# Keys turned inside the recurrence, expert choice and indirect stores inside the mixing

## What is computed

```python
q, k, v = (short_conv(x @ W.T, w) for W, w in ...)      # four taps, then silu
beta = sigmoid(x @ Wb.T)
q, k = l2norm(q), l2norm(k); v = v * beta; kb = k * beta
A = tril(-(kb @ k.T), -1)                               # chunks of 32 in the reference
T = inverse of (I - A), row by row
u, w = T @ v, T @ kb
# recurrence: u_i = u - w @ S; o = q @ S + tril(q @ k.T) @ u_i; S = S + k.T @ u_i
paths = (short_fir(v), long_fir(v), delta, v)
hmid = gelu([x, mean and variance of each path and head] @ W1.T + b1)
probs = softmax(hmid @ W2.T ...), floored, normed
out = rmsnorm(sum of probs * paths) @ Wo.T
x = layernorm(x + out)
logits = x @ router_w + router_b                        # top 2 of 8, softmax over the two
x = layernorm(x + sum over the two of weight * expert(x))
```

## Time and profile before

| | us |
|---|---|
| median of 3 runs | 1947.79 (1944.25 to 1954.17) |
| profiled execution | 1950.38, span of its instructions 1948.6 |
| middle stage in it | about 240 to 1430 |
| one pair of its loop, 1054.6 to 1190.4 | 135.8 |
| busy in this pair | PE 114.1, DVE 111.9, ACT 73.9, POOL 20.7 |

### The profile page before, as it was taken

The page is one execution under the profiler, slowest core; times in us unless marked ns, Lnnn a source line. Parts: engine busy times, 40 slices in busy tenths (PEclk is TensorE's granted clock), DMA queues, the critical chain, the costliest instruction groups (busy, mean ns, idle before and its releaser), DMA issues. The chain is left out here.

```text
span 1948.6 us, 40303 instructions
## 1 busy us (share of the span) xinstructions
PE 1461.2 (75%) x12217; PEld 1100.7 (56%) x12218; DVE 1352.0 (69%) x3875; ACT 948.0 (49%) x1990; POOL 443.0 (23%) x473
## 2 busy tenths in 40 slices
PE   6776075877979789789789789687419999999800
PEld 3446044746738658567467467485307777777700
DVE  6995064778878887887878888875574444444488
ACT  5771160455545654655555465432344444444434
POOL 5784200000030040130210300302042333333300
PEclk9997585987987988889879879867659999999955
DMA  5548732033253233333333332431535533333295
GB/s 190 193 162 239 185 66 52 12 74 84 58 130 97 63 103 98 88 88 108 85 100 87 110 86 66 108 98 61 168 113 162 160 94 95 96 93 95 74 368 195
DMA packets 297373, 224.36 MB, mean 115 GB/s; under 512 B 173472, under 2 KB 265632, under 8 KB 296960
## 3 DMA queue, kind: packets, MB, share of 16 engines
q1 hardware_dynamic: 225600, 158.84, 28.7%
q0 software_dynamic: 15232, 43.53, 6.2%
q10 hardware_dynamic: 56384, 19.93, 4.4%
HBM read 130.42 MB, written 91.82 MB: 114 GB/s over the span
## 5 line engine op out<-in xcount | busy, mean ns | idle before, releaser
L2019 POOL DMA_INDIRECT y_d<-C_yb,C_dest x136 | 131.6, 968 | 260.1 <-ACT C_yb L2130 257.5
L1443 DVE SCALAR_TENSOR_TENSOR B_conv<-B_ps_x,B_cw,B_conv 128x511 f32<-128x511 f32 (+2 forms) x192 | 143.4, 747 | 39.6 <-ACT B_conv L1161 34.6
L688 POOL MEMSET B_z<- 128x256 f32 (+4 forms) x40 | 5.9, 208 | 699.3 <-DMA B_z<-scr_a 699.3
L422 POOL DMA_INDIRECT xs_d<-x,slot_u x128 | 133.4, 1042 | 135.0 <-DVE m_acc L1845 98.2
L745 PE MATMUL B_ps_x<-B_xa,B_wk 128*128 128x512 f32 x128 | 86.2, 813 | 83.8 <-DVE B_sel L1435 44.9
L2255 DVE TENSOR_TENSOR C_xt_low<-C_ps_x,C_xt_high 128x256 fp32r<-128x256 f32 x136 | 57.7, 425 | 109.5 <-ACT C_xt_high L2114 109.5
L2249 DVE TENSOR_TENSOR C_av<-C_sg,C_ps_g 128x256 f32<-128x256 f32 x136 | 57.3, 421 | 95.4 <-ACT C_sg L2124 95.4
L1161 ACT ACTIVATE B_conv<-B_ps_x,B_cw 128x512 f32<-128x512 f32 x64 | 43.7, 683 | 164.0 <-PE B_ps_x L745 161.9
L2053 PE MATMUL C_ps_g<-C_w_high,C_xt_high 128*128 x272 | 119.6, 440 | 0.3 <-issue 0.3
L2053 PE MATMUL C_ps_g<-C_w_high,C_xt_low 128*128 x272 | 107.9, 397 | 0.0
L2053 PE MATMUL C_ps_g<-C_w_low,C_xt_high 128*128 x272 | 107.0, 394 | 0.0
(11 more groups left out here) (329 smaller groups left out, 4251.3 us busy)
## 6 DMA issues: line engine op xcount, KB each, us to landing
C_xb<-xs_d SPq DMA_DIRECT2D x136, 132.0 KB, 2.1
C_w_high<-y_d SPq DMA_DIRECT2D x12, 1024.0 KB, 14.2
A_band<-fir_long POOLq DMA_DIRECT2D x32, 256.0 KB, 6.1
A_work<-xT SPq DMA_DIRECT2D x16, 512.0 KB, 5.0
v_d<-A_v_tok SPq DMA_DIRECT2D x16, 512.0 KB, 3.5
short_d<-A_sh_tok SPq DMA_DIRECT2D x16, 512.0 KB, 3.2
B_xa<-xT SPq DMA_DIRECT2D x8, 1024.0 KB, 5.5
B_v_tok<-v_d SPq DMA_DIRECT2D x8, 1024.0 KB, 5.6
```

The lines of the kernel that those rows point to most:

```text
L422: pool.indirect_dma_start(t["xs_d"][:, :], bass.IndirectOffsetOnAxis(ap=slot_u[:, c:c + 1], axis=0), x1[:, b, j, :], None).then_inc(done, 16)
L1443: V.scalar_tensor_tensor(conv[:, g % 2, k:], X[g % 2][:, :SEQ - k], cw[:, g // 4, gg % CH, 3 - k:4 - k], conv[:, g % 2, k:], ALU.mult, ALU ...
L2019: pool.indirect_dma_start(t["y_d"][:, :], bass.IndirectOffsetOnAxis(ap=dest[:, q:q + 1], axis=0), yb[:, u], None).then_inc(y_out[u], 16)
```

## The change

On TensorE, `stage1b` is cut up. `first_keys` (transposes of keys 0 and 1, transposed norms) and `other_keys` (keys 2 and 3) go into block 3 of the recurrence, around `solve_rows`; they use the banks TR and B3 instead of TR and B2, and the transposes back use B5 and B2 instead of B5 and B4. The projection of query group 4 leaves block 3 and stands in `stage1b`. The x1 transposes go from block 3 into `stage1b`, one at a time through TR alone, and the router behind the last of them. VectorE and ScalarE follow: the norm and keys stand inside block 3 on VectorE, both query groups 4 and 5 behind the recurrence, `late_rows` behind all four `keep_even`; on ScalarE `apply_norm` is split around the root of the key norms, ahead of `keep_u` of block 3.

`choose` is cut in two: the copy of the logits stays before the second norm, the rest goes into the softmax ahead of the wait for the exp. `place` goes behind the taps in `merge_and_mix`, and TensorE's `rank` behind the first merging level. GpSimd's mask goes ahead of its indirect stores. For the last pair, choice and placing stay where they were; its x1 transposes stand behind the recurrence. Pair 1 is unrolled on TensorE. The diff, cut to its core, shows in this order GpSimd's step, TensorE's stage1b and its recurrence (block 3), ScalarE's recurrence, VectorE's recurrence behind residual(3), and VectorE's softmax and mixing:

```diff
                 def step(i, has_prev, has_next):
                     if has_next:
                         fill_blocks(i + 1)
+                    if has_next:
+                        mask_at(i + 1)
                     if has_prev:
                         scatter(i - 1)
-                    if has_next:
-                        mask_at(i + 1)
...
                 def stage1b(p, last=None):
-                    turn_k(p, 0)
-                    turn_k(p, 1)
-                    turn_norms(p, 0)
-                    project(p, 5)
...
+                    back_keys(p, 0)
+                    back_keys(p, 1)
+                    project(p, 4)
+                    back_keys(p, 2)
+                    back_keys(p, 3)
+                    if last is not None:
+                        turn_x1(last, 0)
+                    project(p, 5)
                     pe.wait_ge(kt_kept, 4 * (p + 1))
-                    for jj in range(2):
-                        a_products(p, jj)
+                    a_products(p, 0)
...
+                    a_products(p, 1)
...
+                    s = TPB - 1
+                    from_state(i, s)
+                    if has_next:
+                        select(i + 1, 2)
+                        select(i + 1, 3)
+                        if has_prev:
+                            pe.wait_ge(ln, LN * (i - 1) + 4)
+                        first_keys(i + 1)
+                    solve_rows(i, s)
+                    if has_next:
+                        other_keys(i + 1)
+                    within(i, s)
...
                     for s in range(1, TPB):
                         if has_next:
                             group_b(i + 1, s)
-                            group_a(i + 1, s + 1)
+                            if s < TPB - 1:
+                                group_a(i + 1, s + 1)
                         if has_prev and s == 3:
-                            keep_x1(i - 1, 0)
+                            apply_norm(i - 1, 0)
+                        if has_next and s == 3:
+                            root_squares(i + 1, 0)
+                        if has_prev and s == 3:
+                            apply_norm(i - 1, 1)
                         keep_u(i, s)
...
                     bn(1, 3)
                     bn(0, 1)
+                    if has_next:
+                        first_keys(i + 1)
                     bn(1, 0)
                     if has_next:
-                        taps_of(i + 1, 4)
+                        other_keys(i + 1)
+                    output(3)
                     dve.wait_ge(r_out, 4 * i + 3)
                     bn(2, 3)
                     bn(1, 1)
-                    output(3)
...
                     V.tensor_tensor(lg[:], lg[:], s32[:].unsqueeze(2).to_broadcast(g3), ALU.subtract).then_inc(sm_dve, 1)
+                    if routes:
+                        choose(i - 1)
                     dve.wait_ge(sm_exp, i + 1)
...
                     if has_after:
                         taps_of(i + 2, 0)
+                    if routes:
+                        place(i - 1)
                     if has_next:
                         merge(i + 1, 0)
```

More of the change, by code:

```diff
@@ L840, in stage1b @@
                     if last is not None:
+                        router(last)
                         turn_routes(last)
@@ L966, in recur @@
                         project_out(i - 1, 1)
-                    for s in range(1, TPB):
+                    for s in range(1, TPB - 1):
                         from_state(i, s)
@@ L1093, in _ @@
                 turn_betas(0)
-                for g in range(1, 5):
+                for g in range(1, 4):
                     project(0, g)
@@ L1128, in _ @@
                 step(0, False, True)
-                with pe.Fori(1, PAIRS - 1) as i:
+                step(1, True, True)
+                with pe.Fori(2, PAIRS - 1) as i:
                     step(i, True, True)
@@ L1135, in _ @@
                     project_out(end, b)
-                for b in range(2):
-                    turn_x1(end, b)
+                for n_ in range(4):
+                    turn_x1(end, n_)
                 router(end)
@@ L1214, in stage1b @@
                         keep_odd(jj)
-                    group_b(p, 4)
+                    if last is not None:
+                        keep_x1(last, 1)
+                    for jj in range(2, 4):
+                        keep_odd(jj)
+                        if jj == 2 and last is not None:
+                            keep_x1(last, 2)
+                    group_b(p, 4)
+                    group_a(p, 6)
+                    if last is not None:
+                        keep_x1(last, 3)
+                    group_b(p, 5)
+                    group_a(p, 7)
                     if last is not None:
                         keep_routes(last)
-                    group_a(p, 6)
-                    for jj in range(2, 4):
-                        keep_odd(jj)
-                    group_b(p, 5)
-                    group_a(p, 7)
                     group_b(p, 6)
@@ L1289, in recur @@
                             root_norm(i - 1)
-                            apply_norm(i - 1)
-                        if has_next and s == 3:
-                            root_squares(i + 1, 0)
-                        if has_prev and s == 3:
-                            keep_x1(i - 1, 1)
+                    if has_prev and not has_next:
+                        for n_ in range(4):
+                            keep_x1(i - 1, n_)
                 def gate(i, b):
@@ L1407, in _ @@
                 root_norm(PAIRS - 1)
-                apply_norm(PAIRS - 1)
-                for b in range(2):
-                    keep_x1(PAIRS - 1, b)
+                apply_norm(PAIRS - 1, 0)
+                apply_norm(PAIRS - 1, 1)
+                for n_ in range(4):
+                    keep_x1(PAIRS - 1, n_)
                 keep_routes(PAIRS - 1)
@@ L1473, in stage1b @@
                     keep_k(p, 3)
-                    taps_of(p, 5)
+                def stage1b(p, last=None, first=False):
+                    taps_of(p, 4)
                     dve.wait_ge(beta_ok, 2 * (p + 1))
@@ L1486, in stage1b @@
                         keep_even(jj)
+                    taps_of(p, 5)
+                    for jj in range(2, 4):
+                        keep_even(jj)
                     if not first:
                         late_rows(p - 1)
-                    for jj in range(2, 4):
-                        keep_even(jj)
                     taps_of(p, 6)
@@ L1497, in stage1b @@
                         stats(p - 1)
-                    if last is not None:
-                        place(last)
                 def solver(p):
@@ L1845, in place @@
                     V.tensor_tensor(m_acc[:], m_acc[:], m_sum[:], ALU.add).then_inc(rt, 1)
-                for g in range(5):
+                for g in range(4):
                     taps_of(0, g)
+                first_keys(0)
+                other_keys(0)
                 stage1b(0, first=True)
@@ L1875, in _ @@
                 scale_norm(end)
+                route_logits(end)
                 choose(end)
```

129 lines of the change are left out of this document (72 added, 57 removed).

## The result

The changed kernel takes 2011.48 us (median of 4 runs, 2007.04 to 2016.81) against 1950.98 us before (4 runs); ratio 1.0314, 95% interval 1.0272 to 1.0357. The forecast was 1974 us, range 1955 to 1996: right in sign, wrong in size, since +26 us were forecast and +60.5 measured. The profiled execution took 2007.04 us, span 2005.3, which is 56.7 us more than the span before.

| stretch | before | after | more | forecast |
|---|---|---|---|---|
| to the logits of pair 0 (start) | 433.0 | 441.7 | 8.7 | 1.7 |
| from there to the logits of pair 6 (six periods) | 820.6 | 856.9 | 36.3 | 18.8 |
| logits of pair 6 to logits of pair 7 (last period) | 119.8 | 125.0 | 5.2 | 2.9 |
| from there to the end | 575.2 | 581.7 | 6.5 | 2.6 |

What follows compares the result with a forecast made beforehand. VectorE, busy about 112 of 136 us a pair, binds except from statistics to exp, where the gate's chain does. Terms 12.5 + 7.8 + 0.7 + 1.0 + 1.4 + 2.6 = 26 us on 1947.8 give 1974 us, range 1955 to 1996.

Steps and rivals of the forecast that it cites:

- Choice, 0: Expert choice moved from the second norm's wait to the exp's wait in the softmax: covered in both places, price 0.
- Placing, 2.2 us a pair: Placing behind the taps: its product held by GpSimd's mask, 2.75 us less 0.5 slack, in each of five loop pairs.
- I take the upper one because the mask's row covers the place by its times: Choice of 2.2 us a pair for placing, with the mask's hold, over 1.0 us without it.
- the slack of 0.5 us on TensorE: TensorE's second merging level started on ScalarE's copy, after VectorE's was done, so 0.5 us of placing's delay is absorbed.
- Stores, 25 us, rows x just in time: The 16 indirect stores in the mixing take 25 us; the reloaded rows x land just in time: 0, with a risk.
- Rival C: The rows x come late because each store is held to 2.2 us, delaying add_out: 1992, chance 0.25.
- Keys, +1.3 us a pair: Keys ahead of row norms and query projections: VectorE's waits go from 2.27 to 3.6 us, 7.8 us over six pairs.
- The start, 1.0 + 0.7 us: 1 us for the first keys, taps 4 no longer hiding the norm; 0.7 us for pair 0 before its loop.
- x1 in one bank, 1.4 + 2.6 us: Transposes and copies alternate: 1.4 us in the last pair behind the recurrence, 2.6 us at the end at the cold clock.
- late rows hide all but 1.4: In the last pair, late rows (bn_stats) cover all but 1.4 of the 5.1 us of x1 transposes behind the recurrence.
- nothing waits but VectorE's own queue: Placing's new place, between the taps and the first merge copy, was taken to delay only what follows on VectorE.

Runs made afterwards that it cites:

- b_routes_late: Kernel before with choice, placing, ranks and indirect stores moved, and the mask made to wait for the third weighing product: 1964.57 us, ratio 1.007.
- b_place_late: Kernel before with only ranks, placing and stores moved, choice left ahead of the second norm, mask waiting for the third weighing product: 1963.31 us, ratio 1.0066.
- b_routes: Kernel before with only choice, placing, ranks and indirect stores moved and the mask ahead of the stores, no added wait on the mask: 1982.48 us, ratio 1.0165.
- a_routes_back: Changed kernel with choice, placing, ranks and indirect stores put back where they were, mask behind the stores: 1982.33 us, ratio 1.0174.
- a_mask_late: Changed kernel with one more wait, so the mask starts only after the third weighing product: 1982.90 us, ratio 1.0173.
- a_warm: Changed kernel with seven matmuls without use in each pair from 1 on, to keep TensorE from falling idle in the mixing: 1999.17 us, ratio 1.0263.
- a_x1_two: Changed kernel with the x1 transposes of the last two pairs in two banks by turns, as before: 1982.98 us, ratio 1.0189.

## Why the prediction was wrong

Forecast were +26 us, measured +60.5. Part by part:

- **Choice, 0**: right, both in place (1.78 us of wait left, 1.6 forecast) and in price (1.3 us between b_routes_late and b_place_late).
- **Placing, 2.2 us a pair**: this is the main step that failed, at "I take the upper one because the mask's row covers the place by its times". The row was of the kernel before, and the mask's time was taken as fixed. But the mask waits for the inverse's round trip, that one for the solver, and the solver starts behind placing, which the same part took away. I had followed what is behind placing in its new place, and not what comes earlier without it in the old. The mechanism was right and the object wrong: not a 0.29 us product held 1.25 us, but a 1.22 us product held 3.6. With the mask put back behind the weighing the term measures 3.1 us a pair (forecast 2.2; hold 1.6 instead of 1.25, and the slack of 0.5 us on TensorE gives nothing back). That slack exists: in pair 5 of b_routes_late the second merging level (L890) starts 18.74 us after the logits, 2.5 later than before, and waits for VectorE's copy. But VectorE's own mixing behind the copy is 3.0 us later, and the first state comes 3.2 us later, so VectorE sets the time there. Of the 26.3 us that the mixing grew, 4 x 3.6 = 14.5 are the held product (pairs 1, 3, 4, 5), 5 x 1.5 = 7.5 placing itself, and some 4.4 the late clock of pair 4 (54.2 us of mixing against 49.8 and 49.9 in pairs 1 and 3). In time, the wait on the mask is worth 28.6 us in the changed kernel and 18 in b_routes. With the 15 of the routing and the 19 of the key half behind that wait this makes 62.6, of which 60.5 are measured.
- **Stores, 25 us, rows x just in time**: right: 1177.53 to 1201.35 is 23.8 us, and no wait at add_out. Rival C did not come.
- **Keys, +1.3 us a pair**: 1.8, mis-sized. The waits on VectorE in pair 6's key part are 0.41 (output), 0.60 (taps 4), 1.17, 0.48 and 0.99 (products) and 0.50 us (taps 7); forecast were 0.7, 1.0, 0.2, 0.5, 0.7 and the norm. Output and taps 7 were missed.
- **The start, 1.0 + 0.7 us**: mis-sized; 8.7 in the trace at the first logits, and 7.5 to 8.6 between the two norms, where it belongs. I had priced the first norm, which comes even earlier (259.6 against 261.2), and had not laid out the query groups 4 to 7 behind the products, where no bn_stats of a pair before fill VectorE.
- **x1 in one bank, 1.4 + 2.6 us**: the last period grew by 5.2 (of which 1.5 was placing's in the forecast) and what follows by 6.5, but the term at the end itself measures 3.1 (forecast 2.6). What failed in the last period is the cover: "late rows hide all but 1.4". From the last residual to the statistics the changed kernel takes 5.5 us more than before (22.5 against 17.0). At the upper clock it would be 2.7 to 3.1 more, as a_routes_back, a_mask_late and a_warm show, and the rest is the clock.
- **TensorE's clock** stood in no term of the sum but that of the end. The wait that the change adds on TensorE (5.25 us for B_rk) wasn't in the prediction at all, which had placing where "nothing waits but VectorE's own queue"; so it didn't ask at which level TensorE then runs either. It is the clock that this wait can cost; the merging level L904 itself waits for VectorE's copy behind it (0.68 us).

## What to carry over

When a step leaves a chain, follow that chain forward as closely as the one that it joins: whatever started behind it now starts earlier, and may meet something that it used to miss. Where two instructions exclude each other and start within a microsecond, write down the two start times and their distance before pricing the change; 0.8 us of distance was all that kept this loop free of 3.6 us in each pair. An ordering that matters is worth one wait: the one on the mask gave back about half of the loss.

## What the hardware showed that I had not expected

- GpSimd's mask (128x4096, 3.83 us) and a VectorE tensor_tensor of two SBUF inputs exclude each other for their whole length, and who goes first was settled between 10.80 and 10.82 us in 70 pairs. In pair 1 of a_warm the mask was there at +9.76 us, while the second product ran, and went ahead of the third, which stood next on VectorE:

```profile
592.88 4.83 POOL L698 TENSOR_SCALAR_AFFINE_SELECT area<-area 128x4096 f32<-128x4096 f32 x1 [40.32 <-DMA area<-scr_xt]
```

```profile
593.94 4.85 DVE L1771 TENSOR_TENSOR B_sh<-B_sh,B_lg 128x1024 f32<-128x1024 f32 x1
```

The taps, scalar_tensor_tensors with one input in PSUM, ran under the mask at their usual 2.31 us for three.

- The Trainium skill ("SBUF — State Buffer", Who interferes with whom) has this exclusion, and the traces agree: 4.85 against 1.22 us, 1.87 against 0.29. It also has tensor_tensor not stalling a DMA that GpSimd issues; the indirect stores took up to 2.00 us beside the weighing products and 0.97 otherwise, so here the trace differs again.
- The 512 KB store scr_xt to HBM took 4.6 us from issue to landing in the kernel before and 2.8 in the changed one (medians), and not through the indirect stores. What makes the difference is open.
- The trace with an edit at the end of the program (a_x1_two) is 16.6 us shorter in parts that the edit doesn't touch, and its four runs, each 20 us or more under the fastest of the changed kernel, fit that. Of the 11.2 us in the six periods, 9.6 are the shorter mixing of pair 1 (product free) and pair 4 (product free, no late clock). Why the race falls out differently is open, and so is the start's 5.4.
